# A graph network's first stage: counting products in three PSUM banks, number rows in SBUF, and waits without a marker

## The reference

```python
# layer 0: x += segment_sum(edge_weight * h[dst], src) @ weight + bias
# layer 1: x += (1 + eps) * h + segment_sum(relu(h[src] + edge_attr), dst)
# layer 2: x += A (A h), A = normalised adjacency with self loops,
#          w = dinv[r] * dinv[c], dinv = rsqrt(degree)
# layer 3: x += segment_sum(h[row] * norm, col) on the same graph
```

## Time and profile before

| | |
|---|---|
| median of 3 runs | 9079.17 us |
| profiled execution: time, span | 9074.16 us, 9072.3 us |
| busy: TensorE matmul, weight load | 6311.8 us (70%), 5439.8 us (60%) |
| VectorE, ScalarE, GpSimd | 5135.0 (57%), 3658.8 (40%), 4155.1 (46%) |
| mean granted TensorE clock | 0.79 of full speed |
| DMA | 1969.31 MB, mean 217 GB/s |

### The profile page before, as it was taken

The page is one execution under the profiler, slowest core; times in us unless marked ns, Lnnn a source line. Parts: engine busy times, 40 slices in busy tenths (PEclk is TensorE's granted clock), DMA queues, the critical chain, the costliest instruction groups (busy, mean ns, idle before and its releaser), DMA issues.

```text
span 9072.3 us, 246452 instructions
## 1 busy us (share of the span) xinstructions
PE 6311.8 (70%) x98024; PEld 5439.8 (60%) x98025; DVE 5135.0 (57%) x7430; ACT 3658.8 (40%) x6626; POOL 4155.1 (46%) x4228
## 2 busy tenths in 40 slices
PE   5555555555555555555555555579999899999999
PEld 4444444444444444444444444468888899999999
DVE  5555555555555555555555555599999911111565
ACT  3444444444444444444444444478888600000000
POOL 2455555555555555555555555568888600000000
PEclk6677666676666667666666676799999999999999
DMA  6666566666666666666665666579999987888998
GB/s 172 186 180 179 177 181 183 183 187 179 190 183 181 177 179 200 182 177 181 191 185 177 185 190 184 162 251 316 316 318 316 306 272 261 283 276 277 283 266 213
DMA packets 1540180, 1969.31 MB, mean 217 GB/s; under 512 B 620045, under 2 KB 1204095, under 8 KB 1538767
## 3 DMA queue, kind: packets, MB, share of 16 engines
q1 hardware_dynamic: 1064800, 1272.38, 47.4%
q10 hardware_dynamic: 374342, 523.47, 18.5%
q0 software_dynamic: 100000, 158.60, 5.6%
HBM read 1335.36 MB, written 618.65 MB: 215 GB/s over the span
## 4 chain that ended last, share of the span: by engine, by line
PE 41%; another core or an unknown queue 17%; issue 13%; DVE 12%; ACT 10%; ACTq 2%; DMA 2%; POOL 2%; SPq 0%; DVEq 0%; POOLq 0%
PE pG L2347 9%; PE pT L2230 7%; PE pG L2374 7%; ACT stg L2585 5%; PE pT L2234 3%; PE pG L2186 3%; DVE doh L1724 2%; PE pT L2347 2%; ACT dfar L2552 2%; PE pR L2347 2%; DVE msum L1936 2%; PE pG L2197 2%; PE pG L2195 1%; PE pG L2311 1%
## 5 line engine op out<-in xcount | busy, mean ns | idle before, releaser
L1420 POOL DMA_INDIRECT recB<-rec,qpos x3125 | 3071.8, 983 | 2782.7 <-PE pT L2230 1376.0
L2230 PE MATMUL pT<-soh,doh 128*128 128x128 bf16 x10600 | 1820.9, 269 | 1608.3 <-ACT stg L2585 1317.4
L2585 ACT CAST stg<-pT 128x512 fp8e4<-128x512 f32 x2650 | 1497.7, 585 | 1977.5 <-PE pT L2230 1147.4
L2230 PEld LDWEIGHTS pT<-soh,doh 128*128 128x128 bf16 x10600 | 1042.5, 118 | 1867.8 <-ACT stg L2585 1421.5
L2234 PE MATMUL pT<-car,qidb 128*128 128x256 fp8e4 x2597 | 932.9, 359 | 32.5 <-issue 32.0
L1732 DVE TENSOR_REDUCE val<-pG 128x5 f32<-128x490 f32 x628 | 417.6, 665 | 878.7 <-PE pG L2197 385.4
L1737 DVE TENSOR_TENSOR rec<-pG,wN 128x480 f32<-128x480 f32 x314 | 206.6, 658 | 1173.2 <-remote 1053.1
L2311 PE MATMUL pG<-mpl,doh 128*128 128x144 bf16 x10388 | 765.9, 227 | 38.6 <-POOL mpl L1471 28.7
L1724 DVE TENSOR_TENSOR doh<-dm,pG 128x2560 bf16<-128x2560 bf16 x530 | 783.7, 1479 | 3.0 <-ACT dm L2671 2.6
L1724 DVE TENSOR_TENSOR doh<-smd,pG 128x2560 bf16<-128x2560 bf16 x530 | 783.4, 1478 | 0.0
L1724 DVE TENSOR_TENSOR soh<-smd,pG 128x1280 bf16<-128x1280 bf16 x530 | 432.5, 816 | 514.9 <-PE pT L2230 376.8
(11 more groups left out here) (265 smaller groups left out, 14180.2 us busy)
## 6 DMA issues: line engine op xcount, KB each, us to landing
recB<-zt ACTq DMA_DIRECT2D x102, 2425.5 KB
brec<-recB SPq DMA_DIRECT2D x477, 495.0 KB
erec<-recB SPq DMA_DIRECT2D x477, 495.0 KB, 5.5
cl<-cA SPq DMA_DIRECT2D x80, 2560.0 KB, 10.9
cA<-stg ACTq DMA_DIRECT2D x530, 320.0 KB
cl<-cA SPq DMA_DIRECT2D x40, 2720.0 KB, 11.2
drow<-dlD SPq DMA_DIRECT2D x157, 640.0 KB
srowB<-srD SPq DMA_DIRECT2D x265, 320.0 KB, 5.9
```

Source lines behind the costliest of these rows:

```text
L1420: p.indirect_dma_start(recF, bass.IndirectOffsetOnAxis(ap=qpos[:, s, c:c + 1], axis=0), rec[:, s, c, :], None).then_inc(s_sc[s], 16)
L2230: ins = t.matmul(bank[:, h * 256 + b * 128:h * 256 + b * 128 + 128], doh[:, o, 2 * e + b, h * 128:(h + 1) * 128], soh[:, o, 2 * e + b, :], ...
L2585: a.copy(stg[:, o, :, e * 256:(e + 1) * 256], B8[6 + (g * 5 + e) % 2][:, :].rearrange("p (h x) -> p h x", h=2), saturate=False).then_inc(e ...
```

## The change

`product_bank(c, e)` gives banks 2, 6 and 7 in turn over all products. A product waits for the cast three before it, and the transpose of smK for all five casts of the tenth bucket. The copies into bank 2 go; one_hots, make_oha and make_hsm read ioc and msk in SBUF. `hold` with a constant value is a plain wait; with a value from a register it stays as it was.

```diff
--- before.py
+++ after.py
@@ -229,7 +229,10 @@
 
         def hold(eng, sem_, val):
 
-            eng.wait_ge(sem_, val).then_inc(s_hold, 1)
+            if isinstance(val, int):
+                eng.wait_ge(sem_, val)
+            else:
+                eng.wait_ge(sem_, val).then_inc(s_hold, 1)
 
         def cols(ap, i, g):
             return ap[:, bass.ds(i * TL + g * G, G)]
@@ -1150,8 +1153,6 @@
         B8 = pG + [pR] + pTf
 
 
-        ioA = B8[2][:, :].bitcast(BF16)[:, 0:256]
-        mskA = B8[2][:, :].bitcast(BF16)[:, 256:256 + 6 * SB].rearrange("p (s t two) -> p s t two", s=3, two=2)
         ioB = B8[3][:, :].bitcast(BF16)[:, 0:256]
         qpB = B8[3][:, :].bitcast(BF16)[:, 256:258]
 
@@ -1280,6 +1281,10 @@
                     place, c0 = xi[i % 2][2][32 * q:32 * q + 32, :, 0:w], h * w
                 eng.dma_start(place, cA[J, i * 256:(i + 1) * 256, c0:c0 + w].rearrange("(f r) c -> r f c", r=32)
                               ).then_inc(l_x[i % 2][s], 16)
+
+        def product_bank(c, e):
+
+            return B8[(2, 6, 7)[(c * 5 + e) % 3]]
 
         def settled(r, J):
 
@@ -1633,8 +1638,6 @@
             ch.put(v.tensor_copy(blk2[:, :, 1], blkb))
             turned(0)
             v.wait_ge(t_cp, copied(11))
-            ch.put(v.tensor_copy(B8[2][:, 0:128], ioc[:, :].bitcast(F32)))
-            ch.put(v.tensor_copy(B8[2][:, 128:128 + 3 * SB], msk[:, :, :, :].rearrange("p s t two -> p (s t two)").bitcast(F32)))
             ch.put(v.tensor_tensor(pcs[:, 0:3 * NK].rearrange("p (k s) -> p k s", s=3),
                                    bsB[:, 0:3 * NK].rearrange("p (k s) -> p k s", s=3), bc(kb, 3), ALU.subtract))
             ch.put(v.memset(pcs[:, 3 * NK:160], 0.0))
@@ -1707,7 +1710,7 @@
 
                 v.tensor_tensor(oha_[:, s, :, :].rearrange("p t (c two) -> p t c two", two=2),
                                 blk2[:, bass.ds(ncol(K, s), SB), :].unsqueeze(2).to_broadcast([128, SB, NB // 2, 2]),
-                                ioA[:, 0:NB].rearrange("p (c two) -> p c two", two=2).unsqueeze(1)
+                                ioc[:, 0:NB].rearrange("p (c two) -> p c two", two=2).unsqueeze(1)
                                 .to_broadcast([128, SB, NB // 2, 2]), ALU.is_equal).then_inc(e_oha, 1)
 
             def make_hsm(K, s):
@@ -1716,7 +1719,7 @@
                 v.tensor_tensor(hsm[0:CT, :, :].rearrange("p t (c two) -> p t c two", two=2),
                                 hs[0:CT, :].rearrange("p (c two) -> p c two", two=2).unsqueeze(1)
                                 .to_broadcast([CT, SB, NB // 2, 2]),
-                                mskA[0:CT, s, :, :].unsqueeze(2).to_broadcast([CT, SB, NB // 2, 2]),
+                                msk[0:CT, s, :, :].unsqueeze(2).to_broadcast([CT, SB, NB // 2, 2]),
                                 ALU.mult).then_inc(e_hm, 1)
 
             def one_hots(out, code, n, w, numbers):
@@ -1770,7 +1773,7 @@
                 o, r = g % 2, g % 5
                 v.wait_ge(e_sm, c + 1)
                 reached(v, e_ca, c * 5 - 5)
-                one_hots(soh[:, o, :, :], smd[:, r, :, 0, :], GB, 128, ioA)
+                one_hots(soh[:, o, :, :], smd[:, r, :, 0, :], GB, 128, ioc)
                 v.wait_ge(l_b[r], K * 64 + (g // 5 * 32 + 32))
                 if last:
                     return
@@ -1781,7 +1784,7 @@
 
                 c = K * JG + g
                 o, r = g % 2, g % 5
-                one_hots(doh[:, o, :, :], smd[:, r, :, 1, :], GB, 256, ioA)
+                one_hots(doh[:, o, :, :], smd[:, r, :, 1, :], GB, 256, ioc)
                 if not isinstance(K, int) or c >= 2:
                     add(K - (g < 2), (g - 2) % JG)
                 if last:
@@ -2223,8 +2226,8 @@
                         ins = sums(b)
                         if b == nbk(g) - 1:
                             ins.then_inc(e_ag, 1)
-                    reached(t, e_cv, c * 5 + (e - 1))
-                    bank = B8[6 + (g * 5 + e) % 2]
+                    reached(t, e_cv, c * 5 + (e - 2))
+                    bank = product_bank(c, e)
                     for h in range(2):
                         for b in range(2):
                             ins = t.matmul(bank[:, h * 256 + b * 128:h * 256 + b * 128 + 128],
@@ -2235,7 +2238,7 @@
                                      start=False, stop=True, skip_group_check=True)
                     ins.then_inc(e_ca, 1)
                 if g == JG - 1:
-                    t.wait_ge(e_cv, c * 5 + 4)
+                    t.wait_ge(e_cv, c * 5 + 5)
                     t.transpose(pTb[0:NB, 0:128], smK[:, 0:NB], qidb[:, :]).then_inc(e_tp, 1)
 
             t.wait_ge(e_q, qm["rings"])
@@ -2583,7 +2586,7 @@
                 for e in range(5):
                     hold(a, e_ca, c * 5 + (e + 1))
                     a.copy(stg[:, o, :, e * 256:(e + 1) * 256],
-                           B8[6 + (g * 5 + e) % 2][:, :].rearrange("p (h x) -> p h x", h=2),
+                           product_bank(c, e)[:, :].rearrange("p (h x) -> p h x", h=2),
                            saturate=False).then_inc(e_cv, 1)
                 hold(a, e_cv, c * 5 + 5)
                 at = a.snap(creg, min_val=0, max_val=NP)
```

## The result

| | us |
|---|---|
| the changed kernel, median of 4 | 8714.65 (8672.46 to 8733.82) |
| the kernel before, median of 4 | 9083.49 (9056.56 to 9093.08) |
| ratio, 95% interval | 0.9592 (0.955 to 0.9634) |
| profiled execution after: time, span | 8672.46, 8670.3 |

What follows compares the result with a forecast made beforehand. The prediction took waits, not any engine, to bound the first stage. Its terms, -243 - 60 + 25 + 30 = -248 us, took 9074 to 8826, said as 8830 us; the range was 8560 to 9240.

Steps and rivals of the forecast that it cites:

- likeliest case: The forecast itself, chance 0.50: a time within 8700 us (third product bank at -380) and 8990 us (GpSimd's term at some 200).
- A: Rival, chance 0.15: larger gain, the bucket loop tightens fully, -380 - 228 us, down to 8466 us; likely place 8580.
- Third bank: TensorE's 520 waits for a cast: three products ready instead of two when a first cast comes late; -243 us, ends 0 and -380.
- transpose: TensorE's transpose of smK waits for the tenth bucket's fifth cast, not its fourth; +25 us, ends 0 and 37.
- Plain waits: ScalarE's waits for products: 0.08 us less a hop without the semaphore add; -60 us, ends 0 and -228.
- SBUF rows: Number rows read from SBUF: VectorE's own time 0, ends +-40 us; GpSimd's delayed scatters +30 us, ends 0 and +410.
- GpSimd's longer scatters: GpSimd scatters wait for one two-SBUF-input VectorE operation each: 410 us more on GpSimd, mean scatter 1115 ns instead of 981.
- rival D: Rival, chance 0.09: blocked GpSimd scatters wait for whole VectorE sequences; +230 to +570 us, about 9470; sign: scatters over 1400 ns.
- The cover: GpSimd's pace waits for products of counts, 1363.5 us or 8.9 per slot, shrink and hide most of the scatters' delay.
- Rival C: Rival, chance 0.13: pacing is no cover, the scatters' delay adds to the path since bucket loading waits; +132 us, 9206 us.
- rival F: Rival, chance 0.03: VectorE's 1331 one-hots wait for GpSimd's scatters in flight; +337 us at worst, 9163 us.
- No change (B): Rival, chance 0.10: DMA traffic sets the chain's unknown-queue and issue shares, TensorE merely waits elsewhere; 9047 to 9101 us.

## Why the prediction came out as it did

The measured time lies in the range and within the likeliest case's own bounds (8700 to 8990), though near its lower one. (The range's lower end was called A's likely place; that is 8580, not 8560, and nothing hangs on it.) By its terms:

**Third bank, -243, with the transpose +25, so -218.** Measured about -200, by the kernel without it on chip 3 against the change on the chips of 9075 to 9083 us. The transpose was not measured by itself. The step was right: the third cast of a late bucket follows at once. Its trace in the waits was larger than forecast: I expected each of TensorE's 520 waits to fall by 0.7 us from 2.47; they are 1.06 us each, and half as many. The whole change took a thousand us of waiting away, and 614 of them are between the kernel without the third bank (895) and the whole change (281). The path won a third of these 614, where I had 64% of 380: that the products agree, 200 and 218, is in part luck.

**Plain waits, -60, and SBUF rows, +30, so -30.** Measured about -165 together. This is the step that failed, by size: the term had a fifth of what was measured. That the pair gains is shown; how the gain is split is not, since no run of one of them alone fell on a chip of the kind of the result. What speaks for the plain waits: their far end was -228, while the SBUF rows had only +-40 us of VectorE's own time to gain with, and VectorE's durations did not change. The hop was right (0.08 forecast, 0.09 found), and a bucket became 0.31 us shorter by its median, three to four hops, but 0.08 by its mean, not one hop. The term may have been mis-sized by how many hops count: I took the 1323 casts that the profile lists as waiting for a product, 2.6 per bucket, and 64% of these. It lists the casts that waited for a "remote" source apart, and these were late products too, each with a hop. That is argued from the traces, not shown by a run. All 2650 casts at 0.09 us and 64% would be 153 us, by my estimate. Another reading, that VectorE no longer disturbs TensorE or ScalarE in PSUM, was named ahead of the runs and is not excluded.

**GpSimd's longer scatters.** I forecast 1115 ns and measured 1226. The added time is 3075 x (1226 - 957) = 827 us with rm and rl's share, where the model gave 410 + 73 = 483. The model let each scatter wait for one operation; the timeline shows waits for five. So rival D's mechanism is real, the long scatters hold most of the added time, and I was wrong to give it so little weight as a mechanism. Its price was 0.59 us on each scatter, 1571 ns. The operations did follow each other as it supposed: by its own formula the runs of this trace give 0.63 us. What it had wrong is that a run always holds a scatter to its end; only 120 of 347 were held so. The 1400 ns that I set as its sign were not reached.

**The cover.** That GpSimd's pace waits would hide most of this was right in kind on the chip of the result: they fell from 1363.5 to 344 us, and the gain stands. That only 30 us of it would show is not borne out. Rival C, where they don't hide it, did not happen there, but every kernel with the SBUF rows shows it on chips 1, 4 and 5, where it costs up to 985 us, not 410. The change itself was not run there; its parts in pairs were, on chip 1. I read the cover off one trace and took it for a property of the kernel. It is a property of the kernel on that chip. That the result fell on a chip of the same kind as the trace is nothing that I foresaw. And even on that kind the cover was not whole: on chip 2, 235 us of scatter time less (the memsets) gave 195 us, and 334 us more (qa moved) cost 125. If the first 750 us of added scatter time cost anything like that, the SBUF rows cost far more than 30 us, and the plain waits, or whatever else gained, brought far more than 165. No run shows how much.

**VectorE doesn't wait for GpSimd (rival F at 0.03).** Right. rm takes 649 ns, doh 1481, at a GpSimd that is busy 72% of the stretch. The Trainium skill (SBUF — State Buffer, Who interferes with whom) says that a Vector instruction with two SBUF inputs contends with GpSimd's reads, and the 5.84 us agree. The Trainium skill (SBUF — State Buffer, Summary: rules for kernel authors) says that of such a pair the second to issue fully blocks until the first has finished. Beside a scatter none of these rows shows that for VectorE. Beside other work of GpSimd it does happen. Behind the last scatter GpSimd makes rm and rl of the last buckets itself, from SBUF (first VectorE, then GpSimd, in the changed kernel):

```profile
5463.92 2.27 DVE L1727 TENSOR_TENSOR doh<-smd,ioc 128x2560 bf16<-128x2560 bf16 x1
...
5463.39 1.45 POOL L1448 TENSOR_TENSOR rl<-rm 128x480 bf16<-128x480 f32 x1
```

Nine doh take 2.27 to 2.40 us there, where with the number row in PSUM each takes 1.48, and GpSimd's rl up to 2.11 for 0.99. There each engine holds up the other. Each trace with SBUF rows and doh in one piece has four to nine such doh of over 1.8 us; the kernel before has none. It is worth about 10 us in all.

**No change (B).** The share of the unknown queue did not grow but fell, 26.7 to 18.1%; "issue" took up 6.6 points, more than the 5.0 that products and casts lost. ("Issue" is time in which an engine of the chain waited for nothing that the profile shows.) So part of the gain did turn into another wait, but not all.

## What to carry to other kernels

Before moving a VectorE operand from PSUM to SBUF, count what GpSimd does beside it: an operation with two SBUF inputs holds up a scatter, and a run of them without a gap can hold it up to the end of the run (here 120 of the 347 scatters asked three or more operations ahead of it). Whether it costs is decided by GpSimd's idle time, and that has to be known on more than one chip: the same change was 4% faster on one and its SBUF rows 13% slower on another. If operands must be in SBUF, a one-column memset between such operations costs next to nothing and gave back 2.3% here and half of a 13% loss there.

## What the runs showed of the chip

I had not expected how far chips differ. This is one kernel, SBUF rows and plain waits with two banks, from 200 to 4400 us, first on chip 1 and then on chip 3 (windows, then waits):

```profile
200.00:4400.00 4200.00, 2331.76 (x35432) 1835.57 (x35428) 2598.36 (x4333) 2092.84 (x4074) 3392.20 (x2599) 0.74 0.67 208
```

```profile
PE pT L2231 <- ACT stg L2586: 1310.8, 236, 26.4
...
ACT smd L2564 <- DMA car<-cA: 1118.4, 55, 27.3
...
POOL recB L1423 <- PE pT L2231: 55.2, 181, 0.3
```

```profile
200.00:4400.00 4200.00, 2364.59 (x31407) 1794.43 (x31406) 2340.64 (x3857) 1873.80 (x3625) 2856.34 (x2312) 0.69 0.61 185
```

```profile
ACT stg L2586 <- remote: 725.2, 176, 15.8
...
DVE val L1733 <- remote: 658.9, 110, 16.4
...
ACT hs L2540 <- remote: 541.1, 95, 16.4
DVE rec L1738 <- remote: 530.8, 91, 19.4
...
POOL recB L1423 <- PE pT L2231: 452.6, 204, 7.5
```

On chip 1 the waits name no "remote" source at all, and the long ones are TensorE's for a cast and ScalarE's for a load; on chip 3 "remote" adds up to over 2400 us on two engines. What they are can be seen by taking each cast with its product: on chip 3, 321 of 2650 casts begin over 1 us after their product's last matmul has ended by the trace and ScalarE is free, 1081 us in sum; on chip 1, 9 casts and 13 us. In the other kernels of chips 1, 4 and 5 there are 13 to 66, with at most 149 us. In the result's own trace of before there are 374, with 1016 us. So what the waits of the casts name "remote" is TensorE's products being reported late, or ended later than the trace has them; VectorE's waits are not taken apart like this. In this row of chip 3, TensorE stood still for 5.53 us without a releaser, and in the view of the DMA traffic from 2630 to 2639 us the 16 engines are at 9 tenths or more for three quarters of it:

```profile
2639.97 0.40 PE L2231 MATMUL pT<-soh,doh 128*128 128x128 bf16 x2 [5.53 <-issue]
```

```profile
DMA  9999999999998999999999999999979621000410
```

That full DMA engines are the cause is not shown. Over 200 to 4400 us of this trace the DMA share is 0.54 during the late waits, below the stretch's 0.61; in the 5 us ahead of them it is 0.64, against 0.51 ahead of the other casts, but in the result's trace of before it is 0.55 against 0.52. Chip 1 moves the same bytes, at a higher rate, without it. Its granted clock is higher too, 0.74 for 0.69, and whether that is a cause or follows from fewer waits is open. Which part of the chip is different stays open; so does why. The late products leave GpSimd spare time on one kind of chip, which it doesn't have on the other; that they are why one change has two answers is argued, not shown by a run.
